# Three router operations and one matmul placed elsewhere in steps 10 to 15 of a recurrent block

## The reference, cut to what matters

```python
# L0: a mixture of experts; every token, no dependence between tokens
shared = (silu(x @ sw1.T) * (x @ sw3.T)) @ sw2.T
s = sigmoid(x @ router_w.T + t_bias)               # 8 experts
topk_idx = top_k(s + router_bias, 2)
gates = s_sel / (sum(s_sel) + 1e-9)                 # combine: [tokens, 8]
out = (shared + sum_e combine[:, e] * (gelu(x @ rw1[e].T) @ rw2[e].T)) / 3
...
# L1 and L2: gated scaling, and a conditioned low-rank MLP with gelu
...
# L3: a GRU over the 512 tokens of each sequence
Z = sigmoid(xz + H @ Whz.T + bhz)
R = sigmoid(xr + H @ Whr.T + bhr)
H_tilda = tanh(xh + (R * H) @ Whh.T + bhh)
H = Z * H + (1 - Z) * H_tilda
Y = H @ Whq.T + bhq
```

## Time and profile before

| what | value |
|---|---|
| median of 3 runs | 1274.97 us (1270.42 to 1276.0) |
| the profiled execution: its own time | 1273.17 us |
| its span, first to last instruction | 1270.7 us |
| PE busy | 1211.0 us, 95% |
| DVE busy | 893.8 us, 70% |
| ACT busy | 444.8 us, 35% |
| mean granted TensorE clock | 0.962 |
| first and last step of the GRU start at | 79 us and 1263 us |

### The profile page before, as it was taken

One profiled execution on the slowest core, in us unless ns is written; L12 is line 12 of the kernel. 1 busy time (PEld: TensorE's weight loads), 2 busy tenths in 40 slices (PEclk: granted clock), 3 DMA queues, 4 the chain that ended last, 5 costly groups with the idle time before them and its releaser, 6 DMA issues.

```text
span 1270.7 us, 53687 instructions
## 1 busy us (share of the span) xinstructions
PE 1211.0 (95%) x22315; PEld 1175.9 (93%) x22316; DVE 893.8 (70%) x5772; ACT 444.8 (35%) x2246; POOL 72.2 (6%) x55
## 2 busy tenths in 40 slices
PE   5899999999999999999999999999999999999975
PEld 5789999999999999999999999999999999999864
DVE  4347777777777777777777777777777777777555
ACT  1023333333333333333333333333333333333322
POOL 3310000000000000000000000000000000000000
PEclk9899999999999999999999999999999999999755
DMA  9511100011010111000011001000110010010000
GB/s 337 207 24 28 28 4 27 28 28 28 29 28 3 28 28 28 28 28 28 4 28 28 28 28 28 28 11 20 29 28 28 28 28 9 22 28 24 6 6 6
DMA packets 44229, 44.90 MB, mean 35 GB/s; under 512 B 7737, under 2 KB 40769, under 8 KB 42705
## 3 DMA queue, kind: packets, MB, share of 16 engines
q1 hardware_dynamic: 42416, 39.80, 10.6%
q10 hardware_dynamic: 1344, 1.08, 0.3%
q0 software_dynamic: 224, 0.59, 0.2%
HBM read 36.75 MB, written 4.72 MB: 33 GB/s over the span
## 4 chain that ended last, share of the span: by engine, by line
PE 89%; DVE 5%; DMA 2%; ACT 1%; issue 1%; SPq 0%; POOL 0%; DVEq 0%; POOLq 0%
PE bank L379 48%; PE gate_rh L379 31%; PE gate_z L379 10%; DMA gates<-gates_t 1%; DVE state L1006 1%; ACT rg L714 1%; DVE rhp L990 1%; DMA gates_t<-comb_rows 1%; DVE comb L864 1%; DVE scaled L862 1%; DVE comb_rows L868 1%; DMA sw<-in_sw 0%; ACT hin L714 0%; DVE zin L1000 0%; DVE rhp L997 0%
## 5 line engine op out<-in xcount | busy, mean ns | idle before, releaser
L379 PEld LDWEIGHTS gate_rh<-state,whp 128*128 128x128 f16 x6144 | 233.5, 97 | 45.8 <-DVE state L1006 34.2
L379 PE MATMUL gate_rh<-state,whp 128*128 128x8 f16 x6144 | 248.5, 167 | 26.3 <-DVE state L1006 26.3
L714 ACT ACTIVATE rg<-gate_rh 128x16 f32<-128x16 f32 x512 | 94.2, 184 | 479.3 <-PE gate_rh L379 479.3
L379 PEld LDWEIGHTS gate_rh<-rhp,whp 128*128 128x128 f16 x6144 | 231.3, 96 | 16.0 <-DVE rhp L990 10.4
L379 PE MATMUL gate_rh<-rhp,whp 128*128 128x8 f16 x6144 | 236.9, 167 | 7.4 <-DVE rhp L990 7.4
L990 DVE SCALAR_TENSOR_TENSOR rhp<-rg,hist 128x16 f16<-128x16 f32 x512 | 89.7, 175 | 183.2 <-ACT rg L714 179.9
L379 PE MATMUL gate_z<-state,whp 128*128 128x16 f16 x4096 | 180.5, 177 | 0.0
L379 PE MATMUL bank<-ge,rw 128*128 128x128 f32 x1024 | 166.2, 293 | 5.0 <-DVE ge L892 5.0
L714 ACT ACTIVATE zg<-zsum 128x16 f32<-128x16 f32 x512 | 110.6, 216 | 166.9 <-DVE zsum L995 166.9
L379 PE MATMUL bank<-xt,rw 128*128 128x128 f32 x1024 | 159.0, 289 | 2.2 <-DVE sa L873 1.8
L1000 DVE TENSOR_SCALAR zin<-zg,nsscale 128x16 f32<-128x16 f32 x512 | 119.0, 232 | 58.1 <-ACT zg L714 43.6
(11 more groups left out here) (152 smaller groups left out, 1589.3 us busy)
## 6 DMA issues: line engine op xcount, KB each, us to landing
gates<-gates_t SPq DMA_DIRECT2D x30, 512.0 KB, 5.2
aw<-in_aw SPq DMA_DIRECT2D x4, 2048.0 KB, 22.1
xt<-in_xT SPq DMA_DIRECT2D x32, 128.0 KB, 5.2
out<-osb SPq DMA_DIRECT2D x32, 128.0 KB, 3.8
rw<-in_rw SPq DMA_DIRECT2D x2, 1024.0 KB, 11.8
sw<-in_sw SPq DMA_DIRECT2D x3, 512.0 KB, 5.9
gates<-gates_t ACTq DMA_DIRECT2D x2, 512.0 KB, 10.5
wh<-in_wh SPq DMA_DIRECT2D x3, 256.0 KB, 7.9
```

Source lines behind the costliest of these rows:

```text
L379: return pe.matmul(o, w, x, start=start, stop=stop, skip_group_check=True)
L714: return act.activation(o, i, f, **kw)
```

## The change

It moves instructions and adds or removes none. On VectorE, in blocks with router work (0 to 28): operation k = 10 goes from `early` of step 15 to `late` of step 14, operations 11 and 12 go from `late` to `early` of step 15, and 13 stays. On TensorE, in blocks with L0 work (0 to 29): `up_half` is new and issues one filler (one k of a chunk). The last filler of `up_chunks` of step 10 goes into step 11, and one `l0_out` filler of each step behind it goes on to the next, so that steps 10 to 15 hold 6, 5, 5, 5, 5, 4 fillers before and 5 each after. `ex03_done` is now raised in step 11 ahead of H.

```diff
+            def up_half(ps_, w, par, c, k, done, last):
+                i = mm(ps_[:, c % 4 * TOK:(c % 4 + 1) * TOK], w[:, k, c * P:(c + 1) * P], xt[:, par, k],
+                       k == 0, k == KC - 1)
+                if last:
+                    i.then_inc(done, 1)
...
                     if s == 11:
+                        up_half(A1, rw1, par, 3, 1, ex03_done, True)
                         pe.wait_ge(gs_done, count(m2, 1))
-                        l0_out(0, "s", (0, 1), start=True)
+                        l0_out(0, "s", (0,), start=True)
...
                     if s == 14:
-                        l0_out(1, "r", (7,))
+                        l0_out(1, "r", (6, 7))
                         pe.wait_ge(ge03_done, count(m2, 1))
-                        l0_out(0, "r", (0,))
                     if s == 15:
-                        l0_out(1, "r", (0, 1))
+                        l0_out(0, "r", (3,))
+                        l0_out(1, "r", (0,))
...
                     if s == 10:
-                        up_chunks(A1, rw1, par, (2, 3), ex03_done, True)
+                        up_chunks(A1, rw1, par, (2,), ex03_done, False)
+                        up_half(A1, rw1, par, 3, 0, ex03_done, False)
...
                     if s == 15:
-                        l0_out(1, "r", (2, 3), done=l0_done)
+                        l0_out(1, "r", (1, 2, 3), done=l0_done)
...
-                    for at, k in ((11, 4), (14, 8), (14, 9), (15, 10)):
+                    for at, k in ((11, 4), (14, 8), (14, 9), (15, 11), (15, 12)):
...
-                    for at, k in ((7, 0), ..., (13, 7), (15, 11), (15, 12), (15, 13)):
+                    for at, k in ((7, 0), ..., (13, 7), (14, 10), (15, 13)):
```

More of the change, by code:

```diff
@@ L511, in between_z_h @@
                     if s == 11:
+                        up_half(A1, rw1, par, 3, 1, ex03_done, True)
                         pe.wait_ge(gs_done, count(m2, 1))
-                        l0_out(0, "s", (0, 1), start=True)
+                        l0_out(0, "s", (0,), start=True)
                     if s == 12:
-                        l0_out(1, "s", (1, 2))
+                        l0_out(1, "s", (0, 1))
                     if s == 13:
-                        l0_out(0, "r", (6, 7))
+                        l0_out(0, "r", (5, 6))
                     if s == 14:
-                        l0_out(1, "r", (7,))
+                        l0_out(1, "r", (6, 7))
                         pe.wait_ge(ge03_done, count(m2, 1))
-                        l0_out(0, "r", (0,))
                     if s == 15:
-                        l0_out(1, "r", (0, 1))
+                        l0_out(0, "r", (3,))
+                        l0_out(1, "r", (0,))
                 if has_router and s == 4:
@@ L567, in between_steps @@
                     if s == 10:
-                        up_chunks(A1, rw1, par, (2, 3), ex03_done, True)
+                        up_chunks(A1, rw1, par, (2,), ex03_done, False)
+                        up_half(A1, rw1, par, 3, 0, ex03_done, False)
                     if s == 11:
-                        l0_out(0, "s", (2, 3))
-                        l0_out(1, "s", (0,))
+                        l0_out(0, "s", (1, 2, 3))
                     if s == 12:
-                        l0_out(1, "s", (3,))
+                        l0_out(1, "s", (2, 3))
                         pe.wait_ge(ge47_done, count(m2, 1))
-                        l0_out(0, "r", (4, 5))
+                        l0_out(0, "r", (4,))
                     if s == 13:
-                        l0_out(1, "r", (4, 5, 6))
+                        l0_out(0, "r", (7,))
+                        l0_out(1, "r", (4, 5))
                     if s == 14:
-                        l0_out(0, "r", (1, 2, 3))
+                        l0_out(0, "r", (0, 1, 2))
                     if s == 15:
-                        l0_out(1, "r", (2, 3), done=l0_done)
+                        l0_out(1, "r", (1, 2, 3), done=l0_done)
             def body(m, par, has_y, has_l23, has_l0, has_router):
@@ L976, in late @@
                 if has_router:
-                    for at, k in ((7, 0), (8, 1), (9, 2), (10, 3), (11, 5), (12, 6), (13, 7), (15, 11), (15, 12), (15, 13)):
+                    for at, k in ((7, 0), (8, 1), (9, 2), (10, 3), (11, 5), (12, 6), (13, 7), (14, 10), (15, 13)):
                         if s == at:
```

## The result

The changed kernel takes 1256.22 us (median of 4 runs, 1255.64 to 1256.91) against 1274.81 (1270.42 to 1276.0) for the kernel before: ratio 0.9864, 95% interval 0.9845 to 0.9883.

The account below looks back on a forecast made before the run. The prediction took steps 10 to 15 as bound by fillers, the serial chain or, in step 15, VectorE. Gains of 12.2 + 4.2 = 16.4 us gave 1256.8 from the profiled execution, 1258.6 from the median; it predicted 1258, range 1253 to 1264.

Parts of the forecast that it names:

- The bound: Steps 10 to 15 of a block: step 10 bound by fillers, 11 to 14 balanced, 15 bound by VectorE at 2.60 us.
- the 30 waits of the earlier trace: TensorE's waits for VectorE's scan over blocks 0 to 28: 13.2 us in all, read as one per router-work block.
- The router part: Moving router operations on VectorE in steps 14 and 15 cuts step 15 from 2.60 to 2.18: 12.2 us over 29 blocks.
- The detour: In step 15 `scaled`, `comb` and the transpose run ahead of `zin`, which starts 0.47 us later than in step 12.
- The matmul part: Taking one filler out of step 10 on TensorE gives 0.14 us in each of 30 blocks, 4.2 us.
- The covers: Waits in steps 0, 11, 14 and 15 that hide the moved or shifted VectorE work, some with 0.04 to 0.10 to spare.
- The rival that VectorE does not overlap: Operations ahead of `zin` in steps 14 and 15 run without overlap: 4.6 us less gain, 1262 to 1263; chance 0.13.
- The sum: Over the whole kernel, 12.2 and 4.2 us of gain make 16.4 us.
- The rival of the tail: In block 30 the clock falls a few steps later, giving a time of 1252 to 1255 us; chance 0.04.
- The rival of a fall in the middle: The clock falls in steps 10 to 15 mid-kernel, making it slower: 1280 at 55 steps at the lower level; chance 0.03.
- its price of 0.39 us a step: Loss per step at the lower clock, from block 30's 6.2 us in 16 steps; 42 such steps eat 16.4 us.

Follow-up runs that it names:

- the run of that part alone: The kernel before with only TensorE's filler queue changed, so that steps 10 to 15 hold five each, and the router's operations as before: 1267.04 us, ratio 0.9946.

## Why the prediction was right, point by point

**The bound.** That steps 10 to 15 are of three kinds was right, and each kind was tested: taking a filler from a five-filler step changes nothing, giving one to a step that waits for VectorE changes nothing, and of the steps whose fillers were changed only the six-filler step got shorter. One reading was off: the 30 waits of the earlier trace rows are not one for each of the 29 blocks with router work, but these 29 and one in block 0 that has nothing to do with the router.

**The router part** was put at 0.42 us in each of 29 blocks. Step 15 fell from 2.60 to 2.18; over blocks 1 to 28 that step gave 11.6 us, 0.413 each. Alone it gave 11.6 in that step too. The detour belongs to `scaled` and `comb` ahead of the transpose; operation 10 had no share.

**The matmul part** was put at 0.14 in each of 30. It is 0.135 by the steps of the run of that part alone (step 10 0.169 less, step 11 0.034 more). In the full change steps 10 and 11 have 2.149 and 2.188, so it is 0.127. Over blocks 1 to 28 the parts give 11.8 and 3.7 alone, 15.5 in sum, and 14.8 together, so they add up but for 0.7 us.

**The covers.** All held: 0.04 and 0.05 us ahead of `zin` in steps 14 and 15, 0.10 ahead of `rhp` in step 15, 0.08 in step 11, and `finish_l0` ahead of `rhp` in step 0. The size of the last was off: it starts 0.07 later than before and not 0.13. Its input must be ready sooner after the step's start than y's is; why, no run shows. The runs showed how thin the first is: with `comb` there as well, step 15 is 0.09 longer.

**The rival that VectorE does not overlap.** By the rule that the prediction takes from the Trainium skill, "VectorE: DVE Perf Modes", section "The DRAIN you can't avoid", `zin` would have been late in steps 14 and 15. Both are 2.18, and the rows of the run with `comb` late have one operation start 0.08 before the other's end. The measurement decides against the rule as the prediction gives it, for small operations that don't wait for one another. The prediction left out that the same section of the Trainium skill goes on to say that a next operation which is not held starts earlier; these rows are in line with that. The other half, that a semaphore costs nothing, holds where the wait is long over: the transpose of the changed kernel starts 0.09 behind the low part (515.17 to 515.26) though it waits for `comb`. Where one operation waits for the very one in front, the overlap is lost: 0.26 from `comb` to the transpose.

**The sum and the ends.** The sum, 16.4, compares with 16.6 of span in the two profiled executions, but not term by term: 14.8 + 0.5 + 0.1 = 15.4 us are the change's, 2.3 came from block 30, 0.2 from the setup, and block 0's clock took 1.3 back. The medians differ by 18.6, which the interval of the ratio (14.9 to 19.8 us on 1274.8) spans. So it is in part luck that 16.4 and 16.6 lie so close, and the time came out 1.8 below the 1258 predicted though the change gave 1.0 less than its sum. The rival of the tail came true for those 2.3 us. The kernel before is also known less sharply than a difference of two medians suggests: it took 1268.2 to 1277.1 us over its 21 runs, and its medians on the chips of the experiments were 1273.6 and 1273.2. What in the 18.6 is above 15.4 I can't assign to the change: over the eleven traces the setup took between 77.1 and 80.8 us and, where nothing was put into it, block 30 between 40.0 and 43.0.

**The price of a fall of the clock.** The rival of a fall in the middle did not come true, PEclk is 1.00 over blocks 1 to 29, but its price of 0.39 us a step was too low. It was an average over block 30, where many steps lie near 2.2 us at either level. In block 0 of the changed kernel the clock is at its lower level for 3.4 us; steps 1 and 2, which are full of fillers, take 3.29 and 2.67 there, against 2.35 and 2.32 in the kernel before. That is 1.3 us, so by estimate some 43 us at the lower level, and not the 42 steps of the prediction, would have eaten its 16.4 us.

## What to carry to other kernels

In a serial chain with fillers, look at the length of each link and not at busy shares: the longest step here had the least matmul work, and its cause was three small operations ahead of the one on the path. Before moving an operation, read how long the wait is that will cover it, from the start of the operation in front to the start of the one that waits; a cover of 0.35 us held one chained router operation and not two. A filler of 0.22 us was worth 0.17 in the fullest step, where the chain then took over, and nothing in a balanced one, so move fillers from full steps into slack, and stop where the chain takes over.

## What was not expected of the hardware

TensorE's granted clock fell to the lower of its levels, 1.2 GHz, in block 30 in every trace without useless fillers. In the changed kernel it had been busy for 7.4 of the 9.1 us of that block ahead of the fall, and in neither kernel is a gap between the matmuls of block 30 longer than 0.6 us. Fillers that compute nothing of use kept it at 2.4 GHz and made the kernel 6 us faster.

The float32 matmuls of y read columns that lie 8 bytes apart, in runs of eight, and they cost more: their weight loads start 0.117 us apart, in step 0 eight of them take 0.05 us longer than with the identity (0.111 apart), and that shows in the step. That the identity is mostly zeros is not the reason, since the float32 loads of the other fillers, whose operands are data, are 0.110 to 0.111 apart as well. That it is the distance of the columns is the reading left; no run varied it alone.
